# Scatters of routed rows: pairs paced by signals of the working chunks, in place of quarters that wait for landings

## The chip, the cores and the metric

The kernel runs on one core of one Trainium2 chip. The metric is the device time of one execution in microseconds (us); three executions of the kernel before are shown. The core has engines that run side by side, each with its own instruction stream, and that meet only through semaphores: PE (TensorE, matrix products), DVE (VectorE), ACT (ScalarE), POOL (GpSimd) and SP (SyncE, which here only starts DMAs). DMAs are moved by 16 DMA engines. A DMA that POOL starts has its descriptors written by POOL itself, which the profile shows as busy time of POOL; the time from then to the arrival of the data is not POOL's.

## The reference, cut to what matters

One layer of attention without softmax, then one layer of experts with two choices per token and a capacity. There are 8192 tokens (128 batches of 64) of 128 features.

```python
x = x + xattn(layernorm(x), ctx, ctx)          # keys and values normed by head, 16 heads of 8
# ffn(layernorm(x)), T = 8192 tokens, e = 8 experts
capacity = math.ceil(T / e * 1.25)             # 1280 slots per expert
weights = softmax(x_flat @ W_router.T + b_router)
top_vals, top_idx = top_k(weights, 2)
# each expert takes the first 1280 tokens, in token order, that chose it
inputs_tokens = x_flat[used_tokens] * mask
hmid = relu(einsum('ceh,ehi->cei', inputs_tokens, experts_inter))
out = einsum('cei,eih->ceh', hmid, experts_out) * inputs_weights
combined = zeros((T, h)).at[used_tokens].add(out)
x = x + combined
```

The router's bias is drawn wide, so that experts fill up early: once all eight are full, later tokens are sent nowhere.

## The kernel before, in words

The work has two stages.

**Stage 1** goes through the 8192 tokens in 16 chunks of 512 tokens, with a software pipeline: `STEPS` runs s from -1 to 18, and in step s the engines work on chunk s+1 (statistics, projection of keys and values, turning of the normed x), chunk s (norms of keys), chunk s-1 (the state, the attention product, the residual) and chunk s-2 (routing logits). The order inside each engine is written out by hand. Each engine increments a semaphore as it ends a part of a chunk, and `after(engine, sem, number)` waits until the part of chunk `number` is done. The ones that matter here are `x_turned` (PE turned the normed x of a chunk), `kv_copied` (ACT copied its keys and values), `state_summed` (PE summed the state), `attended` (PE's attention product), `x1_made` (DVE's residual, L571, which writes the rows) and `place_ready` (DVE's L693: the slot numbers of a unit's tokens are known).

Routing works in **units**: chunk 0, chunk 1, and then pairs of chunks; there are nine, numbered 0 to 8. Each token has a row of 144 numbers (its features, its gates, its number), and each row must go to two slots of a table in DRAM, `slots_dram`, in which each expert has 1280 slots. POOL does this with indirect DMAs, **scatters** (L353), each of which sends 128 rows to 128 slots: 8 scatters for a unit of one chunk, 16 for one of two chunks. They are cut in **quarters** of 4 scatters. Before each quarter but the first, POOL waits until the quarter before it has landed. Units 6, 7 and 8 may find all experts full: for unit 6 and 7 POOL first reads a count (`fewest`) and skips the scatters if no expert has a free slot; after the scatters of such a unit it waits for the last quarter to land. For unit 8 it waits first for all earlier scatters and for DVE's last count (`last_counted`, L649), and then raises `slots_ready`. In this data units 0 to 6 are sent (96 scatters) and 7 and 8 are skipped.

DVE waits for scatters in two places: the residual of chunk a overwrites the rows of chunk a-8, and the places of unit u overwrite those of unit u-4.

**Stage 2** takes the 8 experts in turn, each with its 1280 slots in 5 groups of 256. SP waits for `slots_ready`, loads the slots of expert 0 in two pieces (the first 256 slots, L284, and the rest, L285), and then goes on to further experts as buffers come free. For each group PE turns the rows (L896), ACT and DVE split them in two parts (L479, L765), PE multiplies by the first weights (from L908), ACT and DVE take the ReLU apart (L483, L779), PE multiplies by the second weights, ACT applies the gates (L493), and POOL adds the results into the output with indirect DMAs of 128 rows (L393), 10 for each expert. Between experts POOL waits until the adds of the one before have landed (`rows_added`).

Of the kernel before, what the change touches and what calls it, by code (L numbers as in the profile page):

```python
# [20 lines left out]
G = 4  # L21
# [20 lines left out]
PG = PAIR * P  # L42
QUARTER = 4
STEPS = range(-1, CHUNKS + 3)


def valid(chunk):
    return 0 <= chunk < CHUNKS
# [11 lines left out]

def quarters(u):
    return UNITS[u][1] * G * TOP_K // QUARTER

# [36 lines left out]
def build(nc, x, ctx_t, wq_t, bq, wkv_t, bkv, wr_t, br, w_in, w_out, out, slots):  # L100
    with ExitStack() as stack:
# [112 lines left out]
        ct_loaded = [sem(f"ct_loaded{b}") for b in range(RING)]  # L214
        rows_sent = [[sem(f"rows_sent{u}_{q}") for q in range(quarters(u))] for u in range(LAST + 1)]
        x1_stored = [sem(f"x1_stored{b}") for b in range(ROWS_RING)]
# [98 lines left out]
        def _(pool):  # L315
# [29 lines left out]
            pool.drain().then_inc(pads_cleared, 1)  # L345

            def scatter(u):
                first, number = UNITS[u]
                for j in range(number * G * TOP_K):
                    c, q = first + j // (G * TOP_K), j // QUARTER  # L350
                    if j % QUARTER == 0 and q > 0:
                        pool.wait_ge(rows_sent[u][q - 1], 16 * QUARTER)
                    pool.indirect_dma_start(  # L353
                        slots[:, :], bass.IndirectOffsetOnAxis(ap=place_no[:, u % PLACES_RING, j:j + 1], axis=0),
                        rows[:, c % ROWS_RING, j // TOP_K % G, :], None, bounds_check=SLOTS - 1, oob_is_err=False,
                    ).then_inc(rows_sent[u][q], 16)

            for u in range(LAST + 1):
                if not may_be_full(u):
                    after(pool, place_ready, u)  # L360
                    scatter(u)
                elif u < LAST:
                    after(pool, place_ready, u)
                    least = pool.value_load(fewest[0:1, u:u + 1])
                    with pool.If(least < CAPACITY):
                        scatter(u)
                        pool.wait_ge(rows_sent[u][-1], 16 * QUARTER)
                else:
                    for w in range(LAST + 1):
                        if not may_be_full(w):  # L370
                            pool.wait_ge(rows_sent[w][-1], 16 * QUARTER)
                    pool.wait_ge(last_counted, 1)
                    least = pool.value_load(fewest[0:1, u:u + 1])
                    with pool.If(least < CAPACITY):
                        after(pool, place_ready, u)
                        scatter(u)
                        pool.wait_ge(rows_sent[u][-1], 16 * QUARTER)
                        pool.sem_inc(slots_ready, 1)
                    with pool.Else():
                        pool.sem_inc(slots_ready, 1)  # L380
# [120 lines left out]
        def _(dve):  # L501
# [64 lines left out]
            def residual(a):  # L566
                after(dve, attended, a)
                if a >= ROWS_RING:
                    dve.wait_ge(x1_stored[a % ROWS_RING], 16)
                    dve.wait_ge(rows_sent[unit_of(a - ROWS_RING)][-1], 16 * QUARTER)  # L570
                dve.tensor_tensor(rows[:, a % ROWS_RING, :, 0:D], x_sb[:, a % RING], ps_o, ALU.add).then_inc(x1_made, 1)  # L571
# [44 lines left out]
            def step(s):  # L616
# [69 lines left out]
                if p2 is not None:  # L686
# [3 lines left out]
                    if p2 >= PLACES_RING:  # L690

                        dve.wait_ge(rows_sent[p2 - PLACES_RING][-1], 16 * QUARTER)
                    dve.tensor_tensor(place_no[:, p2 % PLACES_RING, 0:columns],  # L693
# [268 lines left out]
```

## Time and profile before

| | |
|---|---|
| three runs | 413.33, 415.86 and 410.4 us, median 413.33 |
| profiled execution, device time | 408.41 us |
| its span, from the first to the last instruction | 406.7 us |
| mean granted TensorE clock | 0.852 of full speed |
| busy share: PE, DVE, ACT, POOL | 71%, 56%, 52%, 54% |
| scatters of rows (L353) | 96, POOL busy 94.1 us |
| adds to the output (L393) | 80, POOL busy 123.4 us |

The span is the part of the profiled execution in which instructions run; 1.7 us lie around it. Busy shares are means over two stages that are bounded by different things, so they say little by themselves: each stage is to be read for itself. The profiled execution is a little faster than all three runs.

### The profile page before, as it was taken

How to read it: one execution, taken by the hardware profiler on the slowest of the kernel's cores; microseconds unless marked ns; L12 is line 12 of the kernel's file. 1: busy time of each engine (PE TensorE's matmuls, PEld its weight loads, DVE VectorE, ACT ScalarE, POOL GpSimd, SP SyncE). 2: the span in 40 equal slices, each digit the busy share in tenths (PEclk: the TensorE clock that was granted, in tenths of full speed). 3: DMA queues.
4: the chain of work that ended last, by engine and by line, in shares of the span. 5: the costliest groups of instructions: out<-in, count | busy, mean ns of one | idle time of the engine just before them, and what ended most of it. 6: DMA issues, size and time to landing. Idle time of an engine off the chain costs nothing. (4 is left out here: it accounts for less than half of the span.)

```text
span 406.7 us, 6739 instructions
## 1 busy us (share of the span) xinstructions
PE 289.4 (71%) x2205; PEld 242.7 (60%) x2205; DVE 225.9 (56%) x892; ACT 211.4 (52%) x431; POOL 221.0 (54%) x197
## 2 busy tenths in 40 slices
PE   1679889897979797771005999999999896971000
PEld 0456566675756565551004999999999896970000
DVE  3477997979797979666002655555555452530000
ACT  3367858585858575622002676767676554650000
POOL 3000266354636666556640383868668686858681
PEclk9989888898989898856556999999999996997555
DMA  5103744243434442211006356374664542423341
GB/s 178 62 2 103 204 120 131 91 130 112 134 106 121 126 130 67 80 50 30 10 0 188 108 72 145 34 157 78 114 146 38 101 39 26 39 28 33 27 38 13
DMA packets 50707, 34.68 MB, mean 85 GB/s; under 512 B 4701, under 2 KB 46298, under 8 KB 50672
## 3 DMA queue, kind: packets, MB, share of 16 engines
q1 hardware_dynamic: 35120, 22.75, 19.7%
q0 software_dynamic: 14592, 11.16, 18.7%
q10 hardware_dynamic: 960, 0.33, 0.3%
q8 instruction: 18, 0.29, 0.3%
q14 instruction: 17, 0.14, 0.1%
HBM read 18.82 MB, written 16.58 MB: 87 GB/s over the span
## 5 line engine op out<-in xcount | busy, mean ns | idle before, releaser
L393 POOL DMA_INDIRECT out_dram<-y_sb,token x80 | 123.4, 1543 | 64.0 <-issue 37.4
L353 POOL DMA_INDIRECT slots_dram<-rows,place_no x96 | 94.1, 980 | 112.7 <-DVE place_no L693 50.0
L779 DVE SCALAR_TENSOR_TENSOR hid_lo<-ps,hid_hi 128x1024 fp32r<-128x1024 f32 x40 | 49.0, 1224 | 57.0 <-ACT hid_hi L483 57.0
L483 ACT ACTIVATE hid_hi<-ps 128x1024 fp32r<-128x1024 f32 x40 | 41.2, 1029 | 36.7 <-PE ps L910 36.7
L859 PE MATMUL ps<-wkv_sb,ct_sb 128*128 128x256 f32 x128 | 53.1, 516 | 6.4 <-DMA ct_sb<-ctx_t_dram 5.4
L908 PE MATMUL ps<-xgt_hi,wi_hi 128*128 128x256 f32 x160 | 49.2, 308 | 0.0
L929 PE MATMUL ps<-hid_hi,wo_hi 128*128 128x256 f32 x160 | 49.0, 306 | 0.0
L909 PE MATMUL ps<-xgt_lo,wi_hi 128*128 128x256 f32 x160 | 46.0, 287 | 0.0
L910 PE MATMUL ps<-xgt_hi,wi_lo 128*128 128x256 f32 x160 | 45.8, 286 | 0.0
L930 PE MATMUL ps<-hid_lo,wo_hi 128*128 128x256 f32 x160 | 45.4, 284 | 0.0
L931 PE MATMUL ps<-hid_hi,wo_lo 128*128 128x256 f32 x160 | 45.4, 283 | 0.0
L765 DVE TENSOR_TENSOR xgt_lo<-ps,xgt_hi 128x256 fp32r<-128x256 f32 x40 | 16.9, 423 | 40.8 <-ACT xgt_hi L479 40.2
L859 PEld LDWEIGHTS ps<-wkv_sb,ct_sb 128*128 128x128 f32 x128 | 26.6, 257 | 19.3 <-issue 16.9
L896 PE MATMUL ps<-ident,xg 128*128 128x128 f32 x80 | 16.1, 284 | 26.4 <-DMA xg<-slots_dram 26.4
L536 DVE TENSOR_REDUCE ss<-sq 128x128 f32<-128x1024 f32 x16 | 19.5, 1216 | 24.5 <-ACT sq L444 24.5
L441 ACT COPY xnt<-ps 128x512 f32<-128x512 f32 x16 | 9.3, 580 | 43.9 <-PE ps L878 43.9
L839 PEld LDWEIGHTS ps<-wr_mid,x1t 128*128 128x128 f32 x128 | 16.3, 199 | 26.2 <-ACT x1t L452 24.7
L908 PEld LDWEIGHTS ps<-xgt_hi,wi_hi 128*128 128x128 f32 x160 | 31.3, 196 | 0.0
L909 PEld LDWEIGHTS ps<-xgt_lo,wi_hi 128*128 128x128 f32 x160 | 31.3, 196 | 0.0
L479 ACT CAST xgt_hi<-ps 128x256 fp32r<-128x256 f32 x40 | 15.3, 383 | 30.6 <-PE ps L896 30.6
L910 PEld LDWEIGHTS ps<-xgt_hi,wi_lo 128*128 128x128 f32 x160 | 31.2, 195 | 0.0
L930 PEld LDWEIGHTS ps<-hid_lo,wo_hi 128*128 128x128 f32 x160 | 30.8, 193 | 0.0
(118 smaller groups left out, 641.5 us busy)
## 6 DMA issues: line engine op xcount, KB each, us to landing
xg<-slots_dram SPq DMA_DIRECT2D x8, 576.0 KB, 4.7
ct_sb<-ctx_t_dram SPq DMA_DIRECT2D x16, 256.0 KB, 3.8
out_dram<-rows SPq DMA_DIRECT2D x16, 256.0 KB, 2.9
x_sb<-x_dram SPq DMA_DIRECT2D x15, 256.0 KB, 4.0
wi_sb<-w_in_dram SPq DMA_DIRECT2D x8, 256.0 KB, 4.9
wo_sb<-w_out_dram SPq DMA_DIRECT2D x8, 256.0 KB, 5.2
slots_dram<-rows,place_no POOLq DMA_INDIRECT x96, 2.3
out_dram<-y_sb,token POOLq DMA_INDIRECT x80, 3.3
```

The lines of the kernel that those rows point to most:

```text
L353: pool.indirect_dma_start(slots[:, :], bass.IndirectOffsetOnAxis(ap=place_no[:, u % PLACES_RING, j:j + 1], axis=0), rows[:, c % ROWS_RING, ...
L393: pool.indirect_dma_start(out[:, :], bass.IndirectOffsetOnAxis(ap=token[:, e, j:j + 1], axis=0), y_sb[:, e % 2, j, :], None, compute_op=AL ...
L483: act.activation(hid_hi[:, i % 2, :], [ps0, ps1][i % 2][:, :], ACT.Relu).then_inc(hid_high, 1)
L536: order.add(dve.tensor_reduce(ss[:, :, :, :], sq[:, :, :, :].rearrange("p g a (h i) -> p g a h i", i=HD), AX.X, ALU.add), "squares")
L779: dve.scalar_tensor_tensor(hid_lo[:, i % 2, :], [ps0, ps1][i % 2][:, :], 0.0, hid_hi[:, i % 2, :].bitcast(F32), ALU.max, ALU.subtract).the ...
L859: pe.matmul(bank, ct_sb[:, n % RING, P * g:P * (g + 1)], wkv_sb[:, :], start=True, stop=False)
L908: pe.matmul(bank, w_hi, xgt_hi[:, i % 2, :], start=True, stop=False)
L909: pe.matmul(bank, w_hi, xgt_lo[:, i % 2, :], start=False, stop=False)
L910: ins = pe.matmul(bank, w_lo, xgt_hi[:, i % 2, :], start=False, stop=True)
L929: pe.matmul(bank, w_hi, h_hi, start=(k == 0), stop=False)
L930: pe.matmul(bank, w_hi, h_lo, start=False, stop=False)
L931: ins = pe.matmul(bank, w_lo, h_hi, start=False, stop=(k == IT - 1))
```

## The change

The quarters and their semaphores go. Each unit has one semaphore, `rows_sent[u]`, which counts all its scatters, and waits for a landed unit wait for the full count. Inside a unit POOL no longer waits for landings. Instead, before each pair of scatters but the first, it waits for a signal of the pipeline (`keep_pace`): pair 1 for the residual of chunk c (c is the first chunk behind the unit, plus 1), pair 2 for the turned x of chunk c+2, pair 3 for the copied keys and values of c+2, pair 4 for the attention product of c+1, pair 5 for the turned x of c+3, pair 6 for the summed state of c+2, pair 7 for the copied keys and values of c+3; near the end, where there is no such chunk, some pairs wait for a residual instead. Lines behind the new function move down by 24 or 25: L353 becomes L377, L393 becomes L417.

```diff
-QUARTER = 4
-def quarters(u):
-    return UNITS[u][1] * G * TOP_K // QUARTER
+def scatters(u):
+    return UNITS[u][1] * G * TOP_K
...
-        rows_sent = [[sem(f"rows_sent{u}_{q}") for q in range(quarters(u))] for u in range(LAST + 1)]
+        rows_sent = [sem(f"rows_sent{u}") for u in range(LAST + 1)]
...
+            def keep_pace(u, pair):
+                c = sum(UNITS[u]) + 1
+                if pair == 1 and valid(c):
+                    after(pool, x1_made, c)
+                if pair == 2 and valid(c + 2):
+                    after(pool, x_turned, c + 2)
+                if pair == 3 and valid(c + 2):
+                    after(pool, kv_copied, c + 2)
+                if pair == 4 and valid(c + 1):
+                    after(pool, attended, c + 1)
+                if pair == 5:
+                    if valid(c + 3):
+                        after(pool, x_turned, c + 3)
+                    elif valid(c + 1):
+                        after(pool, x1_made, c + 1)
+                if pair == 6 and valid(c + 2):
+                    after(pool, state_summed, c + 2)
+                if pair == 7:
+                    if valid(c + 3):
+                        after(pool, kv_copied, c + 3)
+                    elif valid(c + 2):
+                        after(pool, x1_made, c + 2)
...
             def scatter(u):
                 first, number = UNITS[u]
-                for j in range(number * G * TOP_K):
-                    c, q = first + j // (G * TOP_K), j // QUARTER
-                    if j % QUARTER == 0 and q > 0:
-                        pool.wait_ge(rows_sent[u][q - 1], 16 * QUARTER)
+                for j in range(scatters(u)):
+                    c = first + j // (G * TOP_K)
+                    if j % 2 == 0:
+                        keep_pace(u, j // 2)
                     pool.indirect_dma_start(
...
-                    ).then_inc(rows_sent[u][q], 16)
+                    ).then_inc(rows_sent[u], 16)
...
-                        pool.wait_ge(rows_sent[u][-1], 16 * QUARTER)
+                        pool.wait_ge(rows_sent[u], 16 * scatters(u))
```

The order of the instructions stays the same on every engine; what moves is what POOL waits for. On POOL, the first half of unit 3 (a unit in the middle of stage 1; `rows_sent3_0` is the landing of the unit's first quarter) stood in the kernel before as follows, where x3 means three more alike:

```order
L353 DMA slots_dram<-rows,place_no 10240x144 [waits place_ready]
L353 DMA slots_dram<-rows,place_no 10240x144 x3
L353 DMA slots_dram<-rows,place_no 10240x144 [waits rows_sent3_0]
L353 DMA slots_dram<-rows,place_no 10240x144 x3
L353 DMA slots_dram<-rows,place_no 10240x144 [waits rows_sent3_1]
```

The same place of POOL in the changed kernel:

```order
L377 DMA slots_dram<-rows,place_no 10240x144 [waits place_ready]
L377 DMA slots_dram<-rows,place_no 10240x144
L377 DMA slots_dram<-rows,place_no 10240x144 [waits x1_made]
L377 DMA slots_dram<-rows,place_no 10240x144
L377 DMA slots_dram<-rows,place_no 10240x144 [waits x_turned]
L377 DMA slots_dram<-rows,place_no 10240x144
L377 DMA slots_dram<-rows,place_no 10240x144 [waits kv_copied]
L377 DMA slots_dram<-rows,place_no 10240x144
```

A wait for a landing stood ahead of every fourth scatter, and now a wait for the work on a chunk stands ahead of every second.

On POOL, the end of unit 6 (the last one that is sent) and the test for unit 7 in the kernel before:

```order
L353 DMA slots_dram<-rows,place_no 10240x144 [waits rows_sent6_1]
L353 DMA slots_dram<-rows,place_no 10240x144 x3
L353 DMA slots_dram<-rows,place_no 10240x144 [waits rows_sent6_2]
L353 DMA slots_dram<-rows,place_no 10240x144 x3
L365 UNCONDITIONAL_BRANCH [waits rows_sent6_3]
L364 TENSOR_LOAD fewest [waits place_ready]
L365 COMPARE_AND_BRANCH
```

And in the changed kernel, the last three pairs of unit 6 (the two waits for `x1_made` are for chunks 14 and 15, the last residuals of all):

```order
L377 DMA slots_dram<-rows,place_no 10240x144 [waits x1_made]
L377 DMA slots_dram<-rows,place_no 10240x144
L377 DMA slots_dram<-rows,place_no 10240x144 [waits state_summed]
L377 DMA slots_dram<-rows,place_no 10240x144
L377 DMA slots_dram<-rows,place_no 10240x144 [waits x1_made]
L377 DMA slots_dram<-rows,place_no 10240x144
L389 UNCONDITIONAL_BRANCH [waits rows_sent6]
L388 TENSOR_LOAD fewest [waits place_ready]
L389 COMPARE_AND_BRANCH
```

The one wait for landings that is left in the unit stands behind its last scatter.

## Rows read from the trace of the kernel before

**Rows 1.** Stretches of the span: start:end, length; PE, PEld, DVE, ACT, POOL busy; PEclk; DMA share; GB/s.

```profile
190.00:200.00 10.00, 0.68 (x10) 0.46 (x10) 1.92 (x13) 0.00 (x0) 5.04 (x6) 0.50 0.06 15
200.00:214.00 14.00, 0.00 (x0) 0.00 (x0) 0.00 (x0) 0.00 (x0) 7.42 (x8) 0.50 0.02 2
...
250.00:300.00 50.00, 50.00 (x414) 48.41 (x413) 27.50 (x42) 34.16 (x78) 33.50 (x22) 1.00 0.54 97
```

**Rows 2.** Who waited for whom: total us, times, longest us.

```profile
POOL slots_dram L353 <- DMA slots_dram<-rows,place_no: 39.5, 17, 4.3
...
PE ps L896 <- DMA xg<-slots_dram: 26.4, 2, 24.9
```

**Rows 3.** Timeline where stage 2 takes over: start us, us, engine, line, operation [idle before <-releaser].

```profile
191.10 0.19 PE L882 MATMUL ps<-earlier,ones 128*128 128x8 bf16 x1 [0.61 <-DVE place L661]
...
191.83 0.23 DVE L757 TENSOR_TENSOR filled<-slot_no,ps 128x80 uint32<-128x80 f32 x1
...
210.16 0.97 POOL L353 DMA_INDIRECT slots_dram<-rows,place_no  x1 [0.31 <-issue]
213.75 0.37 SPq L284 DMA_DIRECT2D xg<-slots_dram  x1
...
216.15 0.69 PE L896 MATMUL ps<-ident,xg 128*128 128x128 f32 x2 [24.86 <-DMA xg<-slots_dram]
...
217.27 0.42 DVE L765 TENSOR_TENSOR xgt_lo<-ps,xgt_hi 128x256 fp32r<-128x256 f32 x1 [25.22 <-ACT xgt_hi L479]
...
218.38 0.69 PE L896 MATMUL ps<-ident,xg 128*128 128x128 f32 x2 [1.55 <-DMA xg<-slots_dram]
...
218.72 0.56 PE L908 MATMUL ps<-xgt_hi,wi_hi 128*128 128x256 f32 x1
```

**Rows 4.** POOL's two kinds of DMA: costliest groups, durations (ns min/median/max), median landing us.

```profile
L393 POOL DMA_INDIRECT out_dram<-y_sb,token x80 | 123.4, 1543 | 64.0 <-issue 37.4
...
L353 POOL DMA_INDIRECT slots_dram<-rows,place_no x96: 966/968/1247, 47.8 to 210.2; - x96
...
slots_dram<-rows,place_no POOLq DMA_INDIRECT x96, 2.3
```

**Rows 5.** Timeline of POOL in stage 1.

```profile
47.82 1.16 POOL L353 DMA_INDIRECT slots_dram<-rows,place_no  x1 [43.46 <-DVE place_no L693]
...
78.63 0.97 POOL L353 DMA_INDIRECT slots_dram<-rows,place_no  x1 [6.21 <-DVE place_no L693]
...
115.20 0.97 POOL L353 DMA_INDIRECT slots_dram<-rows,place_no  x1 [4.35 <-DMA slots_dram<-rows,place_no]
```

**Rows 6.** Timeline of DVE: places of units 2, 3 and 6, last residual, last count.

```profile
77.69 0.16 DVE L693 TENSOR_TENSOR place_no<-place_f,first_slot 128x16 int32<-128x16 f32 x1
...
98.08 0.16 DVE L693 TENSOR_TENSOR place_no<-place_f,first_slot 128x16 int32<-128x16 f32 x1
...
159.35 0.32 DVE L693 TENSOR_TENSOR place_no<-place_f,first_slot 128x16 int32<-128x16 f32 x1
...
180.24 0.69 DVE L571 TENSOR_TENSOR rows<-x_sb,ps 128x512 f32<-128x512 f32 x1 [2.59 <-PE ps L849]
...
184.96 0.12 DVE L649 TENSOR_REDUCE fewest<-ps 1x1 int32<-1x8 f32 x1
```

**Rows 7.** Timeline of DVE and POOL at two places where both are at work.

```profile
135.53 0.97 POOL L353 DMA_INDIRECT slots_dram<-rows,place_no  x1 [0.30 <-issue]
...
136.01 0.17 DVE L541 TENSOR_SCALAR ss<-ss 128x128 f32<-128x128 f32 x1
...
158.70 0.97 POOL L353 DMA_INDIRECT slots_dram<-rows,place_no  x1 [0.30 <-issue]
...
159.33 0.34 DVE L687 COPY rows<-token_no 128x8 int32<-128x8 int32 x1
```

**Rows 8.** Timeline of POOL in stage 2: the first and the last of the 80 adds.

```profile
229.70 1.58 POOL L393 DMA_INDIRECT out_dram<-y_sb,token  x1 [18.57 <-ACT y_sb L493]
...
396.99 1.54 POOL L393 DMA_INDIRECT out_dram<-y_sb,token  x1 [0.30 <-issue]
```

More of the change, by code:

```diff
@@ L370, in _ @@
                         if not may_be_full(w):
-                            pool.wait_ge(rows_sent[w][-1], 16 * QUARTER)
+                            pool.wait_ge(rows_sent[w], 16 * scatters(w))
                     pool.wait_ge(last_counted, 1)
@@ L376, in _ @@
                         scatter(u)
-                        pool.wait_ge(rows_sent[u][-1], 16 * QUARTER)
+                        pool.wait_ge(rows_sent[u], 16 * scatters(u))
                         pool.sem_inc(slots_ready, 1)
@@ L569, in residual @@
                     dve.wait_ge(x1_stored[a % ROWS_RING], 16)
-                    dve.wait_ge(rows_sent[unit_of(a - ROWS_RING)][-1], 16 * QUARTER)
+                    w = unit_of(a - ROWS_RING)
+                    dve.wait_ge(rows_sent[w], 16 * scatters(w))
                 dve.tensor_tensor(rows[:, a % ROWS_RING, :, 0:D], x_sb[:, a % RING], ps_o, ALU.add).then_inc(x1_made, 1)
@@ L690, in step @@
                     if p2 >= PLACES_RING:
-                        dve.wait_ge(rows_sent[p2 - PLACES_RING][-1], 16 * QUARTER)
+                        dve.wait_ge(rows_sent[p2 - PLACES_RING], 16 * scatters(p2 - PLACES_RING))
                     dve.tensor_tensor(place_no[:, p2 % PLACES_RING, 0:columns],
```

## The prediction

> **What bounds the kernel now.** I read the busy time by stretches first, because the kernel has two stages. Between 190 and 214 us one sees PE, DVE and ACT fall silent while POOL alone goes on with scatters [rows 1]. The list of waits says what the silence is for: PE waited 26.4 us, twice, for `xg<-slots_dram`, the first load of stage 2, 24.9 us of it in one piece [rows 2]. The timeline of that place gives the whole handover [rows 3]. PE's last instruction of stage 1 starts at 191.10, DVE's at 191.83. The last scatter starts at 210.16 and ends at 211.13. SP issues the load of the slots at 213.75, PE turns the first rows at 216.15 and the next at 218.38, and the first product of stage 2 starts at 218.72. So stage 1 ends with POOL, 20 us after everyone else, and every microsecond taken from POOL's last scatter is a microsecond of the kernel until something else is late.
>
> Why is POOL late? It first gets work at 47.82 [rows 5], and 96 scatters of 0.97 us with 0.30 us between them would take 122 us, to about 170. It loses 39.5 us in 17 waits for landings, at most 4.3 each [rows 2, 5]: the quarters.
>
> Stage 2 is a chain of its own. POOL's 80 adds take 1.54 us and 0.30 us of issue each [rows 4, 8], together 80 x 1.84 = 147.5 us, of the 168.8 us from 229.70 to the end of the last at 398.53. The other 21.3 us lie at the seven changes of expert, 3.0 us each. PE is full up to 300 us [rows 1], but it works ahead of POOL. All of stage 2 hangs on its first product: if that starts earlier, the chain moves as one piece, since loads, products and adds all follow from each other.
>
> **The change part by part.** *The removed waits.* With no wait inside a unit a scatter takes 0.97 + 0.30 = 1.27 us. Units 0 and 1 (8 scatters each) end by about 58 and 69 us, before the places of unit 2 are ready at 77.85, so unit 2 starts at 78.63 as it does now, 0.78 us behind its signal [rows 5, 6]. From there a unit needs 16 x 1.274 = 20.4 us. DVE's places come every 98.08 - 77.69 = 20.4 us [rows 6]. POOL thus just keeps pace with stage 1, one scatter after the other: units 3, 4, 5 and 6 start about 20.4 us after each other, the last at 78.63 + 4 x 20.4 = 160.2, or 0.78 after its places at 159.67, 160.4.
>
> *The added waits.* In unit 6 the 14 scatters of pairs 0 to 6 end at 160.4 + 14 x 1.274 = 178.3. The last pair must wait for the residual of chunk 15, which ends at 180.93 [rows 6]. With the lag of 0.78 it starts at 181.7 and ends at 181.7 + 1.27 + 0.97 = 183.95. In place of 211.13 this is 27.2 us earlier. What earlier pairs may lose to their signals is not added: they have 180.93 + 0.78 - 178.3 = 3.4 us of room. If one pair in each of units 2 to 6 were held by one lag of 0.78, that is 3.9 us, and the end would move by 0.5. Behind the waiting scatter on POOL stand only scatters, the reading of two counts and `slots_ready`. SP waits for the last of these. DVE waits for the landing of unit 2's rows for the residual of chunk 10, much later than unit 2 would have landed; the trace shows no wait of DVE for a landing even now, and each unit lands no later than it does now. The waits themselves are part of the DMA instructions (the order shows no instruction added), so I take them at nothing; there are only scatters behind them to hide them, and the room of 3.4 us covers them.
>
> *The end of stage 1.* From the end of the last scatter to SP's load it takes 213.75 - 211.13 = 2.62 us now: the landing (median 2.3 us [rows 4]), two counts read, two branches. The same gives 183.95 + 2.62 = 186.6. DVE's last count, which POOL also needs, is there at 185.08 [rows 6], so it does not hold this. The first 256 slots arrive 216.15 - 213.75 = 2.4 us later, at 189.0, the rest 218.38 - 213.75 = 4.6 us later, at 191.2.
>
> *What is late next* is PE, which is busy with stage 1 until 191.3 (its count of the experts, 191.10 + 0.19 [rows 3]). Then it turns the first rows, 0.69 us, and the next, which have just arrived: 191.3 to 192.7. ACT and DVE are free at 192.06; DVE's part for the first group ended 217.69 - 216.15 = 1.54 us after PE began to turn it, so now at 192.9. The first product starts at about 193.0 instead of 218.72: **25.7 us earlier**. That is less than the 27.2 us of the last scatter, and 1.1 more than the shift of the first turned rows, since the wait for the rest of the slots (1.55 us [rows 3]) goes too.
>
> *Stage 2* has the same instructions and the same loads. The loads that fall beside the landings at the changes of expert keep their distance, so I leave the 21.3 us as they are. They are the least certain part: if all seven were as short as the landing and branch at the end of stage 1 (2.6 us), 3 us would go.
>
> **The sum.** Profiled execution 408.41 - 25.7 = 382.7 us, the span 406.7 - 25.7 = 381.0. The median of the runs is 1.2% above the profiled execution. 413.33 - 25.7 = 387.6, and 382.7 x 413.33/408.41 = 387.3. I predict **387.5 us**. From the lowest and the highest of the three runs the same sum gives 384.7 and 390.2.
>
> **A price that the trace does show for denser scatters.** DVE and POOL get in each other's way. DVE's copy at 159.33 took 0.34 us and ended at 159.67, just as the scatter at 158.70 ended; the same copy beside no scatter is short. But the DVE instruction at 136.01, which began 0.48 us into the scatter of 135.53, was not held: 0.17 us [rows 7]. So only the last half of a scatter, some 0.47 us, holds such an instruction (0.63 us into it in the first case). Kinds that can be held are the copy L687, and L541 and L611 (both an operation of one tensor with a scalar, from and to SBUF); of these L541 twice and L611 once in two steps stand ahead of DVE's further work without slack, some 18 in the 12 steps with scatters. With a scatter every 1.27 us, 0.47/1.27 = 37% of them are held, for 0.24 us on average: 18 x 0.37 x 0.24 = 1.6 us. Now a scatter runs some 76% as often (96 in 163 us, against 128 that would fit), so 1.2 us of it is there already. I add nothing; if all 18 were held for 0.47, the loss would be 8.5 us. The Trainium skill (SBUF — State Buffer, "SBUF: two separate sides") says that DVE and GpSimd take the shared port pair "for the whole instruction" and the other fully blocks. By that a scatter would hold for its full duration. The row at 136.01 speaks against it for most of the scatter, the row at 159.33 for it in the rest.
>
> **The rivals.** (1) *Held for the whole scatter.* If a scatter holds DVE for its 0.97 us once scatters are dense, 0.97/1.27 = 76% of the 18 are held for 0.49 us on average: 6.7 us, and the end of stage 1 moves by that. 387.5 + 6.7 = **394 us**. For it: in the kernel before, waits for landings left gaps in which DVE could pass. Against it: 136.01. The page just named would have it so.
>
> (2) *POOL is slowed instead.* Scatters last 0.97 us in the median and 1.25 at most [rows 4]. If those that run beside DVE's work, now all of them, took 1.25, then 96 x 0.28 = 27 us would come back and the gain be gone: **413 us**, no change. For it: the longest ones are beside DVE work. Against: so are most of the short ones, the mean is 0.98, and POOL is beside a busy DVE nearly all the time up to 190 us.
>
> (3) *Slower than before.* The same mechanism past that point: descriptors of up to 16 scatters are under way with nobody waiting, so that POOL has to wait for the DMA engines at every scatter. The nearest row for such a scatter is the add of stage 2, 1.54 us with 0.30 [rows 8]. 96 x 1.84 = 177 us from 47.8 is 224.5, 13.4 us after the end now: **426 us**. It decides at 1.25 us per scatter, mean. Against it: a landing takes 2.3 us, so at 1.27 us per scatter only two or three are under way, where a quarter has four now; and the ten adds of an expert follow each other at 0.30 us without a wait.
>
> (4) *The pacing does nothing.* Signals have always passed when POOL comes to them. But for the last pair this is what I expect, and it gives the same time; without that one wait the end of stage 2's preparations would still be set by PE at 191.3.
>
> **How the numbers follow.** The forecast (384 to 391) has a chance of 0.82. Rival 1, or another stretching of stage 1 that leaves a gain of 15 to 22 us: 0.10. Rival 2: 0.04. Rival 3: 0.04. The range reaches from 381 (lowest run, less 3 us at the changes of expert and the rest of a us where PE's first products, now at half clock after the silence, start warmer) to 397 (highest run, plus the 6.7 us of rival 1). It leaves out rivals 2 and 3 and little more. Three runs lie within 1.3% of each other, so that about 2% is what a measurement can tell from no change: faster by over 2% (under 405) holds the forecast and rival 1, 0.92 of the chance; within 2%, 0.04; slower, 0.04.
>
> **What would show it.** Right: the waits of POOL for the landing of scatters are gone but for one; scatters follow each other at 1.27 us from 78.6 us on; the last starts at about 183; SP's load at about 186.6; PE's wait for `xg` shrinks from 24.9 us to under 1; the first product at 193; the last add ends at about 373. Wrong: DVE's L541, L611 and L687 above 0.5 us in the mean, residuals more than 20.5 us apart in two steps (rival 1), scatters whose median is above 1.1 us (rivals 2, 3), or changes of expert that take more than 3.0 us each, which would mean that stage 2 does not move as one piece.

## The result, and the profile after

Four runs of the changed kernel have a median of 422.44 us (419.86 to 423.19), four of the kernel before 414.60 us. The ratio is 1.0213, with a 95% interval of 1.0112 to 1.0314: slower beyond the noise, though not surely by more than 2%, where a gain of 6% was forecast. Ratios, here and in the table below, leave out executions over 1.5% above the fastest of their kernel, so they differ a little from the quotient of the medians (here 1.0189). The profiled execution took 423.0 us, its span is 421.3 us, at a mean granted clock of 0.837.

What the change was to do, it did. The waits of the changed kernel (total us, times, longest us) name no landing of scatters any more, and PEld (the loading of PE's weights) waits 0.3 us for `xg` where PE had 24.9 us in one piece [rows 2]. Other rows are new:

```profile
POOL slots_dram L377 <- DVE place_no L718: 63.8, 3, 43.4
...
PE ps L864 <- ACT x1t L476: 25.1, 8, 6.6
...
ACT x1t L476 <- remote: 19.3, 7, 5.8
...
DVE rows L596 <- remote: 14.4, 4, 5.6
...
PEld ps L921 <- DMA xg<-slots_dram: 0.3, 1, 0.3
```

PE now waits for ACT's copy `x1t`, and ACT and DVE for something "remote": at the moment at which they went on, the profile saw a semaphore change but no instruction end. The handover between the stages (timeline; start us, us, engine, line) answers to [rows 3]:

```profile
220.49 0.69 DVE L596 TENSOR_TENSOR rows<-x_sb,ps 128x512 f32<-128x512 f32 x1 [2.66 <-PE ps L874]
221.95 0.97 POOL L377 DMA_INDIRECT slots_dram<-rows,place_no  x1 [4.95 <-DVE rows L596]
223.22 0.97 POOL L377 DMA_INDIRECT slots_dram<-rows,place_no  x1 [0.30 <-issue]
...
226.83 0.37 SPq L283 DMA_DIRECT2D xg<-slots_dram  x1
...
231.65 1.28 PE L921 MATMUL ps<-ident,xg 128*128 128x128 f32 x4
...
233.33 0.55 PE L933 MATMUL ps<-xgt_hi,wi_hi 128*128 128x256 f32 x1 [0.40 <-DVE xgt_lo L790]
```

The account closes with two differences. From the last residual to the first product of stage 2 it was 218.72 - 180.24 = 38.48 us [rows 3, 6] and is 233.33 - 220.49 = 12.84: a gain of 25.6 us, where 25.7 were forecast. But the last residual itself starts at 220.49 in place of 180.24, so stage 1 lost 40.25 us. Together 14.6 us, which is the difference of the spans (421.3 - 406.7). Stage 2 kept its length: the first product to the end of the last add at 413.17 is 179.84 us, and was 398.53 - 218.72 = 179.81 [rows 3, 8].

Where stage 1 loses, one place shows (timeline of PE and ACT; rows between them left out):

```profile
91.76 0.66 PE L845 MATMUL ps<-ident,rows 128*128 128x128 f32 x4
...
92.25 1.02 PE L853 MATMUL ps<-xnt,wq_sb 128*128 128x512 f32 x2
...
92.36 1.01 ACT L472 COPY kvb<-ps 128x1024 f32<-128x1024 f32 x1
...
96.56 0.59 ACT L476 COPY x1t<-ps 128x512 f32<-128x512 f32 x1 [3.18 <-remote]
...
97.19 1.66 PE L864 MATMUL ps<-wr_mid,x1t 128*128 128x8 f32 x7 [3.92 <-ACT x1t L476]
```

ACT is free at 93.37 and PE's L845, whose product it copies, ended at 92.42. ACT still stands for 3.18 us, and PE then 3.92 us for ACT. The semaphore records of the same trace tell what lies between. L845 and L853 increment their semaphores not when they end but about 4 us later; ACT starts 0.03 us after the record:

```
instruction  end us   increment recorded us   late us
PE L837       51.91   59.15                   7.24
PE L827       91.83   94.40                   2.58
PE L845       92.41   96.53                   4.12
PE L853       93.27   97.25                   3.97
PE L827      205.59  213.99                   8.40
```

Of the increments that have a record, 41 of PE's 275 come more than 0.5 us late, 9 of DVE's 399 and none of ACT's 279. In the trace of the kernel before none did: the largest delay of PE was 0.04 us. That trace holds 5591 semaphore records, this one 3810, for the same number of increments, so records are missing too: mostly of the scatters' landings (some 465 are left of 1536), but also some 94 of DVE's, 41 of ACT's and 21 of PE's, of which nothing can be said here.

### The profile page after: what moved, and what is told of

Same layout as the page of the kernel before. It is cut to its first block and busy times, and to the rows that moved or that the text cites. A ratio compares the mean times of both kernels' runs of the same rounds, so it can differ in the third digit from the quotient of the medians.

```text
span 421.3 us, 6739 instructions
## 1 busy us (share of the span) xinstructions
PE 301.7 (72%) x2205; PEld 253.4 (60%) x2205; DVE 228.2 (54%) x892; ACT 212.3 (50%) x431; POOL 221.2 (52%) x197
## 5 line engine op out<-in xcount | busy, mean ns | idle before, releaser
L377 POOL DMA_INDIRECT slots_dram<-rows,place_no x96 | 94.2, 981 | 125.6 <-DVE place_no L718 63.8
L417 POOL DMA_INDIRECT out_dram<-y_sb,token x80 | 123.5, 1544 | 65.5 <-issue 36.6
L884 PE MATMUL ps<-wkv_sb,ct_sb 128*128 128x256 f32 x128 | 54.0, 524 | 6.4 <-DMA ct_sb<-ctx_t_dram 5.5
L864 PEld LDWEIGHTS ps<-wr_mid,x1t 128*128 128x128 f32 x128 | 22.3, 263 | 50.7 <-ACT x1t L476 33.4
L864 PE MATMUL ps<-wr_mid,x1t 128*128 128x8 f32 x128 | 23.7, 313 | 37.8 <-ACT x1t L476 25.1
L884 PEld LDWEIGHTS ps<-wkv_sb,ct_sb 128*128 128x128 f32 x128 | 27.6, 267 | 20.8 <-issue 18.5
L954 PEld LDWEIGHTS ps<-hid_hi,wo_hi 128*128 128x128 f32 x160 | 30.7, 192 | 0.1
L956 PEld LDWEIGHTS ps<-hid_hi,wo_lo 128*128 128x128 f32 x160 | 30.7, 192 | 0.0
L517 ACT ACTIVATE y_sb<-ps,gate 128x128 f32<-128x128 f32 x80 | 25.0, 369 | 11.0 <-DMA out_dram<-y_sb,token 9.7
```

Source lines behind the costliest of these rows:

```text
L377: pool.indirect_dma_start(slots[:, :], bass.IndirectOffsetOnAxis(ap=place_no[:, u % PLACES_RING, j:j + 1], axis=0), rows[:, c % ROWS_RING, ...
L417: pool.indirect_dma_start(out[:, :], bass.IndirectOffsetOnAxis(ap=token[:, e, j:j + 1], axis=0), y_sb[:, e % 2, j, :], None, compute_op=AL ...
L864: ins = pe.matmul(ps_logit[:, l % 2 * G + g, :], x1t[:, P * g:P * (g + 1)], wr_mid[:, :], start=True, stop=True)
L884: pe.matmul(bank, ct_sb[:, n % RING, P * g:P * (g + 1)], wkv_sb[:, :], start=True, stop=False)
L954: pe.matmul(bank, w_hi, h_hi, start=(k == 0), stop=False)
L956: ins = pe.matmul(bank, w_lo, h_hi, start=False, stop=(k == IT - 1))
```

## The experiments

The two traces thus differ in something that the change could have made (one semaphore a unit, waits on engines' signals, dense rows of scatters) or that could lie outside the kernel. Experiments whose results seemed to contradict each other told these apart, but for the cause of the lateness itself. The table has the 18 that were measured, with the result and the trace of the kernel before, sorted by what their own trace shows. Late are increments of PE over 0.5 us behind the end of their instruction.

```
kernel                                 label  this us before us ratio  95% interval    records late longest
no increment late: "quiet"
 before (trace of the prediction)      -          -      -       -     -                5591    0
 before                                e15    405.75  406.67  0.9950  0.9878-1.0021     5591    0
 changed                               e5     380.06  405.95  0.9373  0.9316-0.9430     5599    0
 no pacing                             e1     379.11  405.05  0.9355  0.9271-0.9439     5591    0
 no pacing, sem. a quarter             e9     379.06  406.93  0.9297  0.9166-0.9428     5583    0
 pacing, sem. a quarter                e4     378.12  405.05  0.9354  0.9265-0.9442     5595    0
 pacing, sem. a quarter                e6     379.86  405.95  0.9367  0.9295-0.9438     5575    0
 pacing, sem. a quarter                e10    378.26  406.93  0.9277  0.9123-0.9432     5596    0
 landing waits, one sem.               e2     405.48  405.05  0.9967  0.9921-1.0014     5592    0
 landing waits, one sem.               e11    406.57  406.93  0.9984  0.9937-1.0032     5587    0
 pacing and landing waits              e3     406.55  405.05  1.0068  1.0027-1.0109     5585    0
 no pacing, memset between             e16    381.70  406.67    -     (378.37, 385.02)  5568    0
 landing waits but in units 5, 6       e17    395.77  406.67  0.9756  0.9581-0.9931     5592    0
 landing waits but in units 5, 6       e18    393.45  406.14  0.9709  0.9599-0.9818     5595    0
increments late: "lagging"
 changed                               result 422.44  414.60  1.0213  1.0112-1.0314     3810   41   8.40
 changed                               e7     418.89  414.10  1.0128  0.9948-1.0308     3888   43   7.77
 no pacing                             e8     458.13  414.10  1.1077  1.0857-1.1297     3783   37  11.81
 no pacing, sem. a quarter             e12    457.13  413.33  1.1107  1.0818-1.1396     3794   38  14.69
 no pacing, landing wait after a unit  e13    458.60  412.47  1.1231  1.1082-1.1380     3772   35  13.65
 pacing and landing waits              e14    415.08  412.47  1.0101  1.0030-1.0172     4069   32   6.69
```

The changed kernel in e7 has two executions, and its interval includes 1: taken alone, e7 does not tell it from the kernel before.

**The parts of the change, one by one.** `e1_no_pace` is the changed kernel without its added waits:

```
-                    if j % 2 == 0:
-                        keep_pace(u, j // 2)
```

> The changed kernel without its pacing: inside a unit POOL waits for nothing, and a unit has one landing semaphore. In the changed kernel updates of semaphores by PE arrive up to 8.4 us after the instruction that makes them (91.83 to 94.40, 92.41 to 96.53), and never in the kernel before. Theory 1, the late updates come from scatters that follow each other with no wait for a landing (more scatters outstanding, more landing updates): still late updates, steps as long as in the changed kernel, 415 to 425 us. Theory 2, they come from POOL waiting for semaphores of other engines: no late updates, and the gain that was predicted, about 388 us. Theory 3, they come from up to 256 landing updates on one semaphore: late updates, 415 to 425 us.

`e2_quarters_one_sem` keeps the landing wait before each quarter and only counts all of a unit on one semaphore:

```
-                    if j % QUARTER == 0 and q > 0:
-                        pool.wait_ge(rows_sent[u][q - 1], 16 * QUARTER)
+                    if j % 4 == 0 and j > 0:
+                        pool.wait_ge(rows_sent[u], 16 * j)
```

> The changed kernel with its pacing replaced by waits for landings at every fourth scatter, as in the kernel before, but counted on the one semaphore of the unit. Theory 1 (no wait for landings) and theory 2 (waits for engines' semaphores): like the kernel before, ratio 0.99 to 1.01. Theory 3 (one semaphore for many landings): late updates and steps as in the changed kernel, ratio 1.02 or more.

`e3_pace_and_quarters` is the kernel before with `keep_pace` added:

```
+                    if j % 2 == 0:
+                        keep_pace(u, j // 2)
                     if j % QUARTER == 0 and q > 0:
```

> The kernel before with the pacing added: pairs wait for the chunks' signals, and quarters still wait for landings on semaphores of their own. Theory 1 and theory 3: like the kernel before, ratio 0.99 to 1.01, since signals have passed when POOL comes to them. Theory 2: late updates and long steps, ratio 1.02 or more.

`e4_pace_quarter_sems` is that without the landing waits inside a unit, so it differs from the changed kernel only in having a semaphore for each quarter:

```
-                    if j % QUARTER == 0 and q > 0:
-                        pool.wait_ge(rows_sent[u][q - 1], 16 * QUARTER)
```

> The changed kernel (pacing, no wait for landings inside a unit) with landing semaphores for each quarter, as before. Theory 1 and 2: as slow as the changed kernel, ratio 1.01 to 1.03. Theory 3: no late updates, and the predicted gain, about 388 us, ratio 0.94.

Measured: 379.11, 405.48, 406.55 and 378.12 us, beside 405.05 for the kernel before. Both kernels without landing waits inside a unit had the gain that was forecast (25.9 and 26.9 us), both with them took the time of before. No part of the change was slow here, so the loss in the result was not yet found, and it was not certain that it belonged to the kernel.

**The changed kernel once more.** `e5_after_again` is it, unaltered; `e6_pace_first_half` repeats the kernel of e4 beside it, as the nearest neighbour.

> The changed kernel, unaltered, on the chip that runs this call. The runs without pacing (e1) and with semaphores for each quarter (e4) each gave the predicted gain, so that neither the dense scatters, nor the pacing, nor the shared semaphore alone makes updates late. If it takes the pacing and the shared semaphore together: late updates again and a ratio of 1.02 or more. If the late updates belong to the chip or the session of the first measurement and not to the program: no late updates, and about 380 us, ratio 0.93 to 0.94.

> The kernel of e4 again (pacing, a landing semaphore for each quarter), beside the changed kernel on the same chip. If the outcome goes with the program: 0.935 again, no late updates. If it goes with the occasion: it falls with the changed kernel, whichever way that goes.

Measured: 380.06 us (377.44 to 382.18, six runs), 42 us under the first measurement of the same program. A handover of stage 1 from PE to DVE, in this trace (timeline):

```profile
115.48 1.03 PE L864 MATMUL ps<-wr_mid,x1t 128*128 128x8 f32 x8 [0.90 <-DVE place L686]
116.75 1.09 PE L874 MATMUL ps<-state,qt 128*64 128x128 f32 x16 [0.23 <-issue]
118.49 0.68 DVE L596 TENSOR_TENSOR rows<-x_sb,ps 128x512 f32<-128x512 f32 x1
```

L874 is followed by the residual 0.65 us after its end. In the first trace of the changed kernel the same pair reads

```profile
112.41 1.98 PE L874 MATMUL ps<-state,qt 128*64 128x128 f32 x16
...
117.23 0.69 DVE L596 TENSOR_TENSOR rows<-x_sb,ps 128x512 f32<-128x512 f32 x1 [4.62 <-remote]
```

with PE done at 114.39 and its increment recorded at 117.20. The waits of e5 name no "remote" at all. The kernel is the same, the condition is not.

**The two conditions apart.** `e7_after_third` is the changed kernel again, `e8_no_pace_again` the one without pacing, one after the other on one chip.

> The changed kernel, unaltered, on whichever chip this call gets. The first measurement gave 422.4 us with late updates of semaphores in stage 1, e5 gave 380.1 us with none. Theory A, the late updates hang on the occasion (a chip, a core or its surroundings): on an occasion like the first about 420 us beside a kernel before of about 414; on others about 380 beside 405. Theory B, they are a rare state of the program that can come on any chip: now and then a run near 420 among runs near 380.

> The kernel of e1 (no pacing), beside the changed kernel on the same chip. On an occasion on which the changed kernel is slow: slow too (late updates) if scatters that follow each other without a landing between are enough, about 388 us if it takes POOL's waits for the other engines. On an occasion on which it is fast: about 380 us.

This pair met the late increments: 418.89 us, and 458.13 without pacing, 10.8% above the kernel before, the program that was 6.5% under it in e1. Its waits, and its POOL in 40 slices of the span:

```profile
ACT x1t L474 <- remote: 38.4, 7, 8.9
...
DVE scaled L724 <- remote: 31.6, 5, 8.8
...
DVE state L568 <- remote: 18.8, 6, 6.1
```

```profile
POOL 3000650372372471471471004848686876868682
PEclk9999978967866667667865659999999999899555
```

POOL starts a unit's 16 scatters in 20 us, then stands some 13 us for places that come late: stage 1 takes some 33.9 us for two chunks (rows of scatters start at 119.05, 152.73, 186.51 and 220.88) where 20.4 us is its pace. While a row runs, PE's increments lag; when it ends, stage 1 catches up. So the lateness goes with the scatters: all 37 late increments of e8 belong to instructions that ended between the start of a scatter and 2.5 us behind its end. Of the 235 that ended at other times none is late (26 ahead of the first scatter, 37 between rows, 172 behind the last). The same count in the first trace of the changed kernel is 41 late, 36 punctual beside scatters, and none of 198 elsewhere. POOL's 80 adds in stage 2, one every 1.84 us, make none late.

PE itself does not stand still meanwhile, as its timeline in e8 shows:

```profile
131.48 1.98 PE L872 MATMUL ps<-state,qt 128*64 128x128 f32 x16
133.38 1.22 PE L882 MATMUL ps<-wkv_sb,ct_sb 128*128 128x256 f32 x2
...
137.69 0.38 PE L901 MATMUL ps<-ident,xn 128*128 128x128 f32 x2
140.27 0.38 PE L901 MATMUL ps<-ident,xn 128*128 128x128 f32 x2 [2.21 <-issue]
```

The increment of L872 was recorded at 141.81, while PE had worked through the products in between without a gap up to 138.07. PE's recorded increments never overtake each other, here or in the first trace of the changed kernel. In the row of e8 that starts at 85.44, three come at 92.52, 93.98 and 95.38, some 1.4 us apart. Another three come at 108.14, 108.26 and 108.32, once the row has ended (105.50). This looks as if increments stood in a queue that moves slowly while scatters run; what the queue is, no trace says.

**Is it the shared semaphore?** `e9_no_pace_quarter_sems` and `e12_no_pace_quarter_sems` are one kernel (e4 without `keep_pace`); e10 and e11 repeat e4 and e2.

> No pacing and no wait for landings inside a unit, as in e1 and e8, but with a landing semaphore for each quarter. There are two kinds of chip so far: on one the kernel before takes about 405 us and dense scatters about 380, on the other the kernel before takes about 414 us, the changed kernel 419 to 422 and dense scatters 458 (e8). On the second kind: 458 us again if the density of the scatters alone makes updates late; about 388 us and no late updates if it is the many landings on one semaphore. On the first kind: about 380 us whatever the cause.

> Pacing with a landing semaphore for each quarter, as e4. On a chip where the kernel before takes about 414 us: 419 to 422 us with late updates if density is the cause, about 388 us with none if it is the shared semaphore. On a chip where it takes about 405: about 380.

> Waits for landings at each quarter, counted on one semaphore of the unit, as e2. On a chip where the kernel before takes about 414 us: the same as it, with no late updates, if density is the cause; above 420 us with late updates if the shared semaphore is. On a chip where it takes about 405: the same as it.

> As e9: no wait for landings inside a unit, no pacing, a landing semaphore for each quarter. On a chip where the kernel before takes about 414 us: 458 us again (as e8) and late updates if the density of the scatters is the cause, about 388 and none if it is the many landings on one semaphore. On a chip where it takes about 405: about 379.

e9, e10 and e11 met the quiet condition, where nothing tells the theories apart. e12 met the late increments: with a semaphore for each quarter (64 increments on each) it takes 457.13 us, as much as e8 with one for each unit (256 increments), 458.13 us. That many landings share one semaphore is not the cause.

**Is it that POOL waits on engines' signals behind scatters whose landing nobody has waited for?** `e13_dense_then_landing` is e8's kernel with a landing wait behind each unit, ahead of the next unit's signal; `e14_pace_and_quarters` is e3's.

```
                 if not may_be_full(u):
                     after(pool, place_ready, u)
                     scatter(u)
+                    pool.wait_ge(rows_sent[u], 16 * scatters(u))
```

> No pacing and no wait inside a unit (up to 16 scatters in a row), but behind each unit POOL waits for the landing of all its scatters before it waits for the places of the next. Per unit of 16 that is one landing of 2.3 us in place of four. Theory 1 (scatters in long dense rows make updates late): on a chip where the kernel before takes about 414 us, late updates and 440 us or more. Theory 2b (it takes a wait for another engine's semaphore directly behind scatters): no late updates, the last scatter about 15 us earlier than in the kernel before, about 398 us. On a chip where the kernel before takes about 405: about 390 either way.

> The kernel before with the pacing added and landing waits kept, as e3. On a chip where the kernel before takes about 414 us: the same as it with no late updates under theory 1, since the rate of scatters is the old one; late updates and more than 420 us under theory 2b, since the pacing puts waits for PE, DVE and ACT right behind scatters. On a chip where it takes about 405: the same as it.

e13 took 458.60 us, as without the wait: theory 2b fell. In e14 neither theory had it right. With landing waits between quarters 32 increments are late as well, up to 6.69 us, where theory 1 expected none, and the kernel takes 415.08 us, 1% over before (0.3 to 1.7%), where theory 2b expected more than 420. Its waits:

```profile
POOL slots_dram L380 <- DMA slots_dram<-rows,place_no: 40.7, 17, 3.5
...
PE ps L923 <- DMA xg<-slots_dram: 14.1, 2, 12.6
...
ACT xnt L468 <- remote: 7.3, 2, 5.0
...
DVE rows L598 <- remote: 6.2, 3, 2.7
```

PE's longest wait for `xg` is 12.6 us, and was 24.9 [rows 2]. Stage 1 has grown by 15.8 us (its last residual starts at 196.0, and 180.24 before [rows 6]), but it grew into the time that PE would have spent waiting for POOL: the last scatter starts only 4.0 us later, at 214.2. So by these traces the landing waits do two things: they go with less delay (summed lateness of PE and DVE 86 us, where the changed kernel has 148 in its first trace and 131 in e7), and their own cost, POOL's lag at the end, covers what is left.

**The kernel before, the rate, and a version for both.** `e15_before_itself` is the kernel before. `e16_spaced` is e1's kernel with a memset of unread columns behind each scatter:

```
                     ).then_inc(rows_sent[u], 16)
+                    pool.memset(spacer[:, 64 * (16 * u + j):64 * (16 * u + j + 1)], 0.0)
```

`e17_last_units_free` and `e18_last_units_free_again` are the kernel before without the landing waits of units 5 and 6:

```
-                    if j % QUARTER == 0 and q > 0:
+                    if j % QUARTER == 0 and q > 0 and u < 5:
```

> The kernel before, unaltered, traced once more, so that its trace can be compared with the changed kernel's on one chip. If quarters that wait for landings keep engines' semaphore updates punctual, every semaphore increment is recorded (about 5590 records) within 0.5 us of the end of its instruction on any chip, and the time is that of the timed runs of the kernel before. If the late updates come from scatters as such on some chips, then on a chip whose timed runs of the kernel before lie at 412 us or above, some 20 to 40 updates of TensorE come over 0.5 us late, up to 7 us, fewer than 4200 are recorded, and the residuals of stage 1 stand at uneven distances; on a chip whose timed runs lie near 405 us none is late.

> One semaphore per unit and no waits on signals, but behind each scatter a GpSimd memset of 64 columns of a tile that nothing reads (it is work that the reference does not ask for), which sets the scatters some 1.4 to 1.7 us apart in place of 1.27 us. On a chip where the kernel before takes about 405 us: 380 to 395 us, by how much later the last scatter of unit 6 gets. On a chip where it takes 412 us or above: if the number of scatters in a row at 1.27 us makes the late updates, 395 to 430 us with updates late by less than the 11.8 us of the kernel without pacing; if only a row that is never broken by a wait does it, 450 us or more as without pacing.

> The kernel before, but units 5 and 6 do not wait for the landings between their quarters: six waits of 1.9 to 2.2 us idle each go, that is some 4.7 us from unit 5 and 5.3 us from unit 6, and the last scatter ends at about 200.5 in place of 211.1. On a chip where the kernel before takes about 405 us: 393 to 397 us. On a chip where it takes 412 us or above: if dense rows cost time only while stage 1 runs (its last residual is at 180.24, unit 5 starts at 159.97), 400 to 408 us; if dense rows cost the same late too, 412 us or more.

> The kernel before with units 5 and 6 free of their six landing waits, once more: its units 0 to 4 are the kernel before, so where its timed runs of the kernel before lie at 412 us or above, its trace shows whether quarters with landing waits alone have late updates of TensorE (theory: some, up to 7 us, before 160 us), and whether dense rows at the end of stage 1 cost less than the 10 us that they give: 400 to 408 us if so, 412 us or more if not. Where the kernel before takes about 405 us: 393 to 397 us again, and no update over 0.5 us late.

All four met the quiet condition, so none of them answers the question that it was made for. A kernel like e16 with a memset of 256 columns, `e13_spaced`, has no measured time. The memset of e16 takes 0.17 us and slipped into the 0.30 us between two scatters, which now follow at 1.30 in place of 1.27 us; even on a lagging chip it would have tested little. e17 and e18 give what was worked out, 10.9 and 12.7 us less than before: the last scatter starts at 199.3 and 198.8, and PE's wait for `xg` is down to

```profile
PE ps L896 <- DMA xg<-slots_dram: 15.9, 2, 14.4
```

in e17. How this version does on a lagging chip was not seen. It is a candidate, since its dense rows begin only at the end of stage 1, and no more than that; the changed kernel is faster where it is quiet.

## Why the prediction was wrong

The forecast was 387.5 us, the range 381 to 397, and the measurement 422.44. In the quiet condition the same program takes 380.06 us, 25.9 us under the kernel before; 25.7 were forecast. So the sum held in the quiet condition, and the result was measured in the other. The points below are read in e5 (timeline and waits):

```profile
179.49 0.69 DVE L596 TENSOR_TENSOR rows<-x_sb,ps 128x512 f32<-128x512 f32 x1 [2.64 <-PE ps L874]
...
180.96 0.97 POOL L377 DMA_INDIRECT slots_dram<-rows,place_no  x1 [2.08 <-DVE rows L596]
182.23 0.97 POOL L377 DMA_INDIRECT slots_dram<-rows,place_no  x1 [0.30 <-issue]
...
185.82 0.37 SPq L283 DMA_DIRECT2D xg<-slots_dram  x1
...
190.30 1.47 PE L921 MATMUL ps<-ident,xg 128*128 128x128 f32 x4
...
191.98 0.55 PE L933 MATMUL ps<-xgt_hi,wi_hi 128*128 128x256 f32 x1 [0.21 <-DVE xgt_lo L790]
...
203.74 1.58 POOL L417 DMA_INDIRECT out_dram<-y_sb,token  x1 [20.54 <-ACT y_sb L517]
```

```profile
POOL slots_dram L377 <- PE ps L903: 2.5, 4, 1.6
...
POOL slots_dram L377 <- DVE rows L596: 2.1, 1, 2.1
```

- *The removed waits* (1.27 us a scatter, POOL just keeping pace): right. Scatters run at 1.27 us from 150 to 178 us without a gap but 0.30.
- *The added waits*: right. Only the last pair is held for long (2.1 us, by the residual of chunk 15); it starts at 180.96 where 181.7 was forecast, and the last scatter ends at 183.20 (183.95). Of the other signals, PE's L903 cost the most, 2.5 us in four waits, inside the room of 3.4.
- *The end of stage 1*: SP's load at 185.82 (186.6), 2.62 us behind the last scatter, to the hundredth what it was.
- *What is late next*: PE, as said, at 190.30 (191.3); first product at 191.98 (193.0).
- *Stage 2 as one piece*: right. Its 80 adds span 203.74 to 372.31, 168.6 us in place of 168.8; the end was forecast at about 373.
- *Rival 1, held DVE*: did not happen. DVE's operation on `ss`, L565 (L541 before), takes 223 ns in the mean where it took 226; the copy of the tokens L712 (L687) 121 in place of 218.
- *Rival 2, slowed POOL*: the scatter's mean is 984 ns quiet and 981 lagging. *Rival 3, waits for DMA engines*: none; the 426 us that it gave (426.7 by its own terms) are near the result by chance. Its mechanism is not the one that was met, and it had all of the chance of 0.04 that was given to "slower".
- *Rival 4, pacing without effect*: right in the quiet condition (379.11 without, 380.06 and 378.12 with). Wrong in the lagging one, where pacing is worth 36 to 39 us (458 against 419 to 422): it breaks the dense rows, and the longest delay is 8.40 us with it and 14.69 without.

**The step that failed** is under *The removed waits*: "POOL thus just keeps pace with stage 1". It takes DVE's places to come every 20.4 us whatever POOL does. In the measured trace they came 24.0 to 27.7 us apart (timeline of DVE, units 2 to 6):

```profile
87.80 0.16 DVE L718 TENSOR_TENSOR place_no<-place_f,first_slot 128x16 int32<-128x16 f32 x1
...
111.76 0.15 DVE L718 TENSOR_TENSOR place_no<-place_f,first_slot 128x16 int32<-128x16 f32 x1
...
139.50 0.16 DVE L718 TENSOR_TENSOR place_no<-place_f,first_slot 128x16 int32<-128x16 f32 x1
...
164.45 0.15 DVE L718 TENSOR_TENSOR place_no<-place_f,first_slot 128x16 int32<-128x16 f32 x1
...
191.81 0.24 DVE L718 TENSOR_TENSOR place_no<-place_f,first_slot 128x16 int32<-128x16 f32 x1
```

Unit 6 thus started at 194.38 in place of 160.4. The residuals stood up to 17 us apart for one chunk (181.26, 198.22), since stage 1's own handovers between PE, ACT and DVE got slower by up to 8.4 us while scatters ran. The sign that the prediction had named for rival 1, residuals more than 20.5 us apart in two steps, did show (166.06 to 198.22), but not from a held DVE: L565 took 212 ns in the mean. What was missing was the term "what scatters do to other engines' signals": 40.25 us in the profiled execution, against a gain of 25.6.

Could the trace of before have told? Not directly, since it was a quiet one: 5591 records, none late. Its hint was in the times: the profiled execution took 408.41 us, the three timed runs 410.4 to 415.86. The prediction scaled that 1.2% away. Kernels of the quiet group ran beside a before of 405.05 to 406.93, those of the lagging group beside 412.47 to 414.60. By their times the timed runs belonged to the second group, and by its increments the trace belonged to the first.

**What stays open.** Why increments are late beside scatters is not known. Scatters' data is not late: the last packet ended 0.93 us behind the end of its scatter in both conditions, and its landing was recorded 0.25 to 0.4 us after that. Nearly all late increments are PE's; none of ACT's that has a record is late. Whether the condition belongs to a chip is open: chip number 5 was lagging in e12 and quiet in e15, and what else ran on the machine is not on record. That the kernel before itself has late increments in the lagging condition was not traced; its 8 us more there and e14, which has its quarters, speak for it. Whether it is the rate of the scatters or the length of a row was not told apart either. And every execution here comes with its span and granted clock, so all may have been recorded ones: no run here could show whether an execution without any recording lags as well. The Trainium skill (NOTIFIC — the notification-queue block, "7.1 Overflow: three behaviours, one of which stalls the engine") says that when a record queue is full, new records are discarded, the oldest are overwritten, or whoever reports is stalled, by the queue's setting. Lost records are seen here (3810 of some 5590 are left). A stalled engine is not: PE worked on while its increment was held.

## What to carry to other kernels

A wait that only costs may still be a brake on something else: before a burst of GpSimd's DMAs is unleashed beside working engines, compare the end of an instruction with the record of its semaphore in the new trace, not only the idle times. When the timed runs lie a per cent or two above the profiled execution, ask whether they ran under the same conditions, rather than scale one to the other. And where a burst must be dense, put it where the other engines have little left to hand each other: freeing the last two units gave 11 to 13 us in the quiet condition, the only one in which it was tried.

## What was not expected of the hardware

- The same program took 380.06 us on one occasion and 422.44 and 418.89 us on two others, while the kernel before went from 406 to 414 us only. Without pacing it is 379 against 458 us.
- In the lagging condition a TensorE increment came up to 14.69 us after the instruction's end (e12), with 0.01 to 0.04 us usual, and only beside scatters. TensorE worked on meanwhile (e8: 18 records of products between the end of L872 and its increment). Beside the adds of stage 2, 1.84 us apart, none came late.
- The mean granted clock is lower where PE is kept waiting in stage 1: 0.793 and 0.821 in e13 and e8, 0.87 in e1.
